# Slot-attention column sums as half-precision matmuls in three passes

## The reference, cut to what matters

```python
for _ in range(NUM_ITERS):                      # 3
    sn = rmsnorm(slots, slot_norm_w)
    q_proj = sn @ Wq.T
    scores = jnp.einsum('bkd,bmd->bkm', q_proj, k_proj) * SCALE
    attn = jax.nn.softmax(scores, axis=-2)      # over the slots (tokens) k
    attn = attn / (jnp.sum(attn, axis=-1, keepdims=True) + EPS)   # over the context rows m
    updates = jnp.einsum('bkm,bmd->bkd', attn, v_proj)
    slots = gru_cell(updates, slots, gru_wih, gru_whh, gru_bih, gru_bhh)
```

## Time and profile before

| | us |
|---|---|
| median of 3 runs | 910.36 |
| lowest, highest | 908.17, 910.95 |
| the profiled execution's own time | 910.25 |
| its span in the trace | 909.0 |
| PE, DVE, ACT, POOL busy | 879.0, 649.0, 557.5, 365.4 |

### The profile page before, as it was taken

How to read it: one execution, slowest core, us unless ns; L and a number is a source line. 1 busy time by engine, 2 the same in 40 slices (tenths; PEclk the granted TensorE clock), 3 DMA queues, 4 the chain that set the end, 5 groups by cost and what they waited for, 6 DMA issues and landing times. The chain is left out here.

```text
span 909.0 us, 23841 instructions
## 1 busy us (share of the span) xinstructions
PE 879.0 (97%) x8190; PEld 670.8 (74%) x8190; DVE 649.0 (71%) x1839; ACT 557.5 (61%) x1347; POOL 365.4 (40%) x492
## 2 busy tenths in 40 slices
PE   5999999999999999999999999999999999999996
PEld 4777777777777777776666666666788888888864
DVE  4767688777676778667878787769677767776755
ACT  5777877777666677657575654645455545554555
POOL 2333434333323455325444442354534444444433
PEclk9999999999999999999999999999999999999999
DMA  9742434342323241230000000099443332333226
GB/s 320 193 140 94 147 107 153 106 140 94 133 75 123 96 158 49 9 93 1 1 1 2 1 1 2 17 361 409 134 113 50 49 49 44 49 49 48 42 29 191
DMA packets 61584, 88.09 MB, mean 97 GB/s; under 512 B 17279, under 2 KB 46527, under 8 KB 61343
## 3 DMA queue, kind: packets, MB, share of 16 engines
q1 hardware_dynamic: 53439, 75.52, 25.2%
q0 software_dynamic: 7488, 10.27, 7.1%
q10 hardware_dynamic: 544, 0.79, 0.3%
HBM read 56.00 MB, written 30.56 MB: 95 GB/s over the span
## 5 line engine op out<-in xcount | busy, mean ns | idle before, releaser
L2254 PE MATMUL ps<-slots,e 128*128 128x128 f16 x1872 | 189.9, 219 | 2.3 <-DVE xs L2421 2.2
L667 POOL TENSOR_SCALAR prob<-prob,rden 128x128 f32<-128x128 f32 (+1 forms) x256 | 110.6, 448 | 202.6 <-DVE rden L956 202.6
L2254 PEld LDWEIGHTS ps<-slots,e 128*128 x1872 | 152.4, 97 | 35.4 <-issue 5.0
L853 ACT ACTIVATE prob<-prob,nmx 128x128 f32<-128x128 f32 (+1 forms) x256 | 114.1, 450 | 41.6 <-DVE nmx L949 38.9
L2262 PE MATMUL ps<-e,xT 128*128 x312 | 117.3, 378 | 0.0
L2351 ACT ACTIVATE slots<-slots 128x512 f32<-128x512 f32 x78 | 49.0, 630 | 106.9 <-DVE slots L2405 103.1
L31 PE MATMUL ps<-xT,wqkv 128*128 128x256 f16 x768 | 97.2, 278 | 0.6 <-DVE wqkv L936 0.6
L31 PEld LDWEIGHTS ps<-xT,wqkv 128*128 128x128 f16 x768 | 70.9, 99 | 30.5 <-issue 22.2
L2263 PE MATMUL ps<-e,xT 128*128 x312 | 85.0, 273 | 0.0
L1766 POOL DMA_INDIRECT xg<-rows_x,dst x39 | 40.9, 1049 | 106.3 <-DVE mask L2394 103.2
L949 DVE CUSTOM_DVE_ANT_0 prob<-ps,mask 128x128 f32<-128x128 f32 (+1 forms) x256 | 75.9, 353 | 5.0 <-PE ps L747 5.0
(11 more groups left out here) (275 smaller groups left out, 1940.5 us busy)
## 6 DMA issues: line engine op xcount, KB each, us to landing
halves<-parted SPq DMA_DIRECT2D x36, 512.0 KB, 2.9
piece<-in_L_ffn_ew SPq DMA_DIRECT2D x32, 512.0 KB, 4.4
e<-halves SPq DMA_DIRECT2D x16, 1024.0 KB, 15.4
piece<-in_L_ffn_sh_w SPq DMA_DIRECT2D x4, 512.0 KB, 8.8
sw<-halves SPq DMA_DIRECT2D x4, 512.0 KB, 6.7
rows_x<-xs SPq DMA_DIRECT2D x4, 512.0 KB, 7.1
xs<-back_y SPq DMA_DIRECT2D x8, 256.0 KB, 5.9
out<-xs SPq DMA_DIRECT2D x8, 256.0 KB, 2.1
```

The source lines that it names most:

```text
L667: PO.tensor_scalar(prob[m % 3][:, h, r], prob[m % 3][:, h, r], rden[m % 2][:, h, t:t + 1], 1.0, ALU.mult, ALU.mult).then_inc(normed, 1)
L853: SC.activation(p, p, ACT.Exp, bias=nmx[u][:, h, t:t + 1], scale=-1.0, accum_out=den[u][:, h, t:t + 1]).then_inc(exped, 1)
L2254: yield PE.matmul(ps[:, 2 * u + q, (k % 4) * P:(k % 4) * P + P], w[ch][h], xgT[u][j][:, ch, :], start=n == 0, stop=n == 3 * DC - 1)
```

## The change

The column sums of steps 1 to 11 are made from half-precision parts. ACT makes `exh[0]`, the exponentials times 2^15 rounded to float16, in one operation on 120 x 512 (`exponentials_high`), behind the r gate of chunk 0 and before the z gate. DVE makes `exh[1]`, what the rounding left, in one operation with two SBUF inputs (`exponentials_low`), at the head of step n before `reset(n, 0)`. DVE also cuts `grec` in two parts, two small operations more in `denominators`. PE then does 3 products for each of the 4 tiles: 12 one-column float16 matmuls in place of 4 float32 ones. On PE the column sums move from between the two halves of the r gate of chunk 1 to behind it. `cse` takes the scale out again. The counts of `g_exp` and `g_rec` follow. The column sum of step 0 stays as it was.

```diff
--- before.py
+++ after.py
@@ -1200,6 +1200,8 @@
         with ExitStack() as c:
             sh.extend([sb(c, f"s{i}{g}", [P, DC, GT], F16) for i in range(2)] for g in range(2, NG))
             sqh = [sb(c, f"sqs{i}", [P, GT], F16) for i in range(2)]
+            exh = [sb(c, f"ex{i}", [P, GT], F16) for i in range(2)]
+            grech = [sb(c, f"grec{i}", [P, BG], F16) for i in range(2)]
             rr = sb(c, "rr", [P, GT])
             sc = sb(c, "sc", [P, BG, S])
             ex = sb(c, "ex", [P, BG, S])
@@ -1222,6 +1224,21 @@
             g_neg, g_exp, g_rec = (sem(k) for k in ("g_neg", "g_exp", "g_rec"))
             cs_mm, c_eps2, c_rec, c_cut, cb_mm = (sem(k) for k in ("cs_mm", "c_eps2", "c_rec", "c_cut", "cb_mm"))
             SUM_UP = 32.0
+            EX_UP, GREC_UP = 2.0 ** 15, 2.0 ** 8
+            def exponents_made(n):
+                return BG * (n + 1) + max(0, n - 1)
+            def exponents_high(n):
+                return BG * (n + 1) + n
+            def inverted(n):
+                return 5 * n - 3 if n else 0
             an_out, an_hi, an_lo = (sem(k) for k in ("an_out", "an_hi", "an_lo"))
             r_mm, z_mm, hn_mm, xn_mm = (sem(k) for k in ("r_mm", "z_mm", "hn_mm", "xn_mm"))
             tr_out, tz_out, hn_out, nn_out = (sem(k) for k in ("tr_out", "tz_out", "hn_out", "nn_out"))
@@ -1258,15 +1275,22 @@
                     mm.then_inc(sc_mm, 1)
 
                 def column_sums(n):
-                    PE.wait_ge(g_rec, 2 * n + 1)
+                    PE.wait_ge(g_rec, inverted(n) + (5 if n else 1))
+                    if n >= 1:
+                        PE.wait_ge(g_exp, exponents_high(n))
                     if n + 1 < STEPS:
                         PE.wait_ge(r_msq, meaned(n + 1))
                     if n >= 1:
                         PE.wait_ge(c_eps2, n)
                     for t in range(TG):
                         k = t * P // S
-                        mm = PE.matmul(ps[:, 6, TG + t:TG + t + 1], exf[:, t * P:t * P + P], grec[0:M, k:k + 1],
-                                       start=True, stop=True)
+                        if n == 0:
+                            mm = PE.matmul(ps[:, 6, TG + t:TG + t + 1], exf[:, t * P:t * P + P], grec[0:M, k:k + 1],
+                                           start=True, stop=True)
+                        else:
+                            mm = split_matmuls(PE, ps[:, 6, TG + t:TG + t + 1], [
+                                ([exh[i][0:M, t * P:t * P + P] for i in range(2)],
+                                 [grech[i][0:M, k:k + 1] for i in range(2)])])
                     mm.then_inc(cs_mm, 1)
 
                 def sums_along(n):
@@ -1299,10 +1323,10 @@
                     else:
                         PE.wait_ge(tr_out, m)
                     from_hidden(n, 0, ch, False)
+                    PE.wait_ge(an_lo, n + 1)
+                    from_update(n, 0, ch, False).then_inc(r_mm, 1)
                     if ch == 1 and n + 1 < STEPS:
                         column_sums(n + 1)
-                    PE.wait_ge(an_lo, n + 1)
-                    from_update(n, 0, ch, False).then_inc(r_mm, 1)
 
                 def gates_z(n, ch):
                     m = 2 * n + ch
@@ -1396,6 +1420,12 @@
                         SC.activation(ex[0:M, k, :], sc[0:M, k, :], ACT.Exp, bias=gneg[0:M, k:k + 1],
                                       accum_out=gden[0:M, k:k + 1]).then_inc(g_exp, 1)
 
+                def exponentials_high(n):
+                    SC.wait_ge(g_exp, exponents_made(n))
+                    if n >= 2:
+                        SC.wait_ge(cs_mm, n)
+                    SC.mul(exh[0][0:M, :], exf, EX_UP).then_inc(g_exp, 1)
                 def weights(n):
                     SC.wait_ge(an_out, BG * (n + 1))
                     if n >= 2:
@@ -1445,6 +1475,8 @@
                 sums_high(2)
                 for n in range(STEPS):
                     gate_r(n, 0)
+                    if n + 1 < STEPS:
+                        exponentials_high(n + 1)
                     if n == STEPS - 1:
                         norm_high(0)
                     gate_z(n, 0)
@@ -1534,7 +1566,7 @@
                     VE.wait_ge(rr_out, n + 1)
                     VE.wait_ge(sc_mm, n + 1)
                     if n >= 1:
-                        VE.wait_ge(g_exp, BG * n)
+                        VE.wait_ge(g_exp, exponents_made(n - 1))
                     for k in range(BG):
                         VE.tensor_tensor_reduce(sc[0:M, k, :], ps[0:M, 5, k * S:(k + 1) * S],
                                                 rr[0:M, k * S:(k + 1) * S], 1 / WS, LOWEST, ALU.mult, ALU.max,
@@ -1543,18 +1575,32 @@
                     VE.tensor_scalar(gneg[0:M, :], gmx[0:M, :], -1.0, None, ALU.mult).then_inc(g_neg, 1)
 
                 def denominators(n):
-                    VE.wait_ge(g_exp, BG * (n + 1))
+                    VE.wait_ge(g_exp, exponents_made(n))
                     if n >= 1:
                         VE.wait_ge(an_out, BG * n)
                     VE.reciprocal(grec[0:M, :], gden[0:M, :]).then_inc(g_rec, 1)
-                    VE.wait_ge(g_rec, 2 * n + 1)
+                    VE.wait_ge(g_rec, inverted(n) + 1)
                     VE.tensor_scalar(grec_up[0:M, :], grec[0:M, :], SUM_UP, None, ALU.mult).then_inc(g_rec, 1)
+                    if n >= 1:
+                        if n >= 2:
+                            VE.wait_ge(cs_mm, n)
+                        VE.tensor_scalar(grech[0][0:M, :], grec[0:M, :], GREC_UP, None, ALU.mult).then_inc(g_rec, 1)
+                        VE.wait_ge(g_rec, inverted(n) + 3)
+                        VE.scalar_tensor_tensor(grech[1][0:M, :], grec[0:M, :], GREC_UP, grech[0][0:M, :], ALU.mult,
+                                                ALU.subtract).then_inc(g_rec, 1)
+                def exponentials_low(n):
+                    VE.wait_ge(g_exp, exponents_high(n))
+                    if n >= 2:
+                        VE.wait_ge(cs_mm, n)
+                    VE.scalar_tensor_tensor(exh[1][0:M, :], exf, EX_UP, exh[0][0:M, :], ALU.mult,
+                                            ALU.subtract).then_inc(g_rec, 1)
 
                 def column_sums(n):
 
                     VE.wait_ge(cs_mm, n + 1)
-                    VE.tensor_scalar(cse[:, :], ps[:, 6, TG:2 * TG], SUM_UP, SUM_UP * SUM_EPS, ALU.mult,
-                                     ALU.add).then_inc(c_eps2, 1)
+                    VE.tensor_scalar(cse[:, :], ps[:, 6, TG:2 * TG], SUM_UP / (EX_UP * GREC_UP) if n else SUM_UP,
+                                     SUM_UP * SUM_EPS, ALU.mult, ALU.add).then_inc(c_eps2, 1)
                     VE.wait_ge(c_eps2, n + 1)
                     if n >= 1:
                         VE.wait_ge(c_cut, 3 * n)
@@ -1569,7 +1615,7 @@
 
                 def weights(n):
                     VE.wait_ge(cb_mm, n + 1)
-                    VE.wait_ge(g_rec, 2 * (n + 1))
+                    VE.wait_ge(g_rec, inverted(n) + 2)
                     if n >= 1:
                         VE.wait_ge(an_hi, n)
                         VE.wait_ge(an_lo, n)
@@ -1626,6 +1672,8 @@
                 sums_low(2)
                 mean_square(2)
                 for n in range(STEPS):
+                    if n + 1 < STEPS:
+                        exponentials_low(n + 1)
                     if n == STEPS - 1:
                         norm_low(0)
                     reset(n, 0)
```

## The result

| | median us | lowest, highest | runs |
|---|---|---|---|
| before | 909.85 | 908.17, 911.94 | 15 |
| changed | 913.50 | 910.55, 915.16 | 15 |

Ratio 1.0039, 95% interval 1.0031 to 1.0047: the change makes the kernel slower by 3.6 us, where +1.35 was forecast. The profiled execution of the changed kernel took 910.88 us (span 909.5), one of its fastest; before's took 910.25.

The account below looks back on a forecast made before the run. A ring of ACT, DVE and POOL, 15.27 us a step, bounds the kernel, not PE. 910.25 - 0.25 + 0.45 + 1.15 = 911.6 us; own range 910.1 to 913.5, set to 907.3 to 915.5 for scatter.

Parts of the forecast that it names:

- What sets the pace: Slot steps: a chain of ACT, DVE and POOL, period 15.27 us, sets the pace; PE follows with 0.3 us to spare.
- the ring: Closed chain of ACT, DVE and POOL operations from one step's z gate to the next, no matmul in it; 15.27 us.
- PE's wait for L470: At `root_along` each step: PE's saved 0.49 us becomes waiting, 0.78 us where it was 0.3.
- Rival 1: PE sets the pace after all, so all 11 savings count: -5.4 us, 904.9 us; chance 0.11.
- PE's slot: Column sum on PE each step: twelve one-column matmuls take 0.32 us instead of 0.81, saving 0.49.
- Step 0: PE bounds step 0, so there the column-sum saving counts: -0.25 us.
- The push on reset: In step 0, `exponentials_low(1)` ahead of reset(0, 0) pushes it by 0.1 to 0.2 us.
- `exponentials_low` behind the power: Steps 1 to 9: POOL's power L462 delays this DVE operation, pushing reset 0.05 us a step: +0.45 us.
- Rival 2: Steps 1 to 9: POOL's power keeps DVE out of SBUF until it ends, +0.61 a step; 916.7 us, chance 0.17.
- Step 10: Later `cse` puts L1567 behind POOL's dl, where it stands and delays `norm_sum(0)` and PE: +1.15 us.
- rival 3: Step 10: L1567 is not held, as dl shifts too or an on-time DVE candidate moves it; 910.6 us, chance 0.14.
- the wait of PE in step 11: PE's 1.04 us wait for POOL's L1500 grows, as all of step 10's 1.15 us delay arrives at PE.

Follow-up runs that it names:

- four_more: The kernel before with 4 more unused one-column float16 matmuls ahead of the float32 column sums of steps 0 to 9; ratio to before 1.0036.
- old_place_10: The changed kernel with step 10's column sum back between the halves of the r gate; 910.20 us, ratio to before 1.0008.
- filled_wait: The changed kernel with 18 unused 256-column matmuls where PE waits 2.5 us in step 11; 910.99 us, ratio to before 1.0015.
- the three padded kernels: 80 or 256 waits heading PE's list in before (1.0012; 256 one run), 80 in the half-precision kernel with slots - nn on DVE (0.9927).
- the two kernels with the shorter chain: slots - nn of steps 0 to 10 on DVE, not POOL: on before (ratio 0.9994), and on the changed kernel with step 10's old order (0.9934).

## Why the prediction came out as it did

What sets the pace: right. The period stayed at 15.27 in every kernel in which dl is made by POOL, with 0.5 us less on PE (changed), with 0.1 more (four_more), and it moved only when the ring was shortened. PE's wait for L470 grew by 0.50 us a step, for a saving of 0.50 (0.49 was forecast). Rival 1 is out.

PE's slot: 0.31 for 0.32, so a one-column pair takes 0.31 / 12, about 26 ns. The prediction took the 8-column row for the nearest one, which was a misreading: the kernel before has one-column float16 matmuls at L441, eight of them in 0.20 us (478.10 to 478.30), 25 ns each. The 81 ns that the Trainium skill ("TensorE: Matmul & The Clock Gate", section "Back-to-back issue gap") has for 128 columns, and that would have given 0.97, was not for this case: the table of the same section has about 25 ns for 1 to 64 columns, and the trace agrees.

Step 0: -0.44 us on the start of step 1's z gate, for -0.25. The push on reset that I had allowed for did not show.

`exponentials_low` behind the power: the term of 0.45 us was too large, it is 0. L1596 took 0.69 with the power in flight. Rival 2 is out. The rule on which it rested (the Trainium skill, "SBUF — State Buffer", section "Who interferes with whom") agrees with dl against L470 (1.23 us for 4 elements) and not with the power. The cast, which has one SBUF input and not two, was held by dl as well (1.09).

Step 10: its period grew by 1.06 us for a forecast of +1.15, but by another instruction, so that the size came out right by luck in part. I had L1567 stand; it was the cast two operations before it. And rival 3 had it wrong that a candidate on time would spare the block: it was on time, dl moved ahead with it, and the block came. In before the 0.46 us gap had held dl back just far enough.

The sum of these is +0.6 us in the traces (S 176.28 to 176.84), not +1.35, and the measurement is +3.6. So the sum had two terms too few. One is shown: the wait of PE in step 11, which I priced at its own length only, is in most executions followed by 3.4 us at half clock, 1.6 us more. old_place_10 and filled_wait take it away by two different edits and gain 3.1 and 2.3 us. In the profile before, had the row (PE idle 1.04 us, to become 2.2) and I did not ask what a longer idle time does to the clock. The other is X, 1.1 us longer in the changed kernel, 0.8 of it in G. The prediction had no term for a stage that the change does not touch. There the fetch of a 16 KB piece on q8 falls at 1.94 us and not 3.59, into the gather, whose last packets come 0.7 us later. Edits of PE's list alone (four_more and the three padded kernels) moved the fetch, and the end of the gather with it. That the gather's last packets stand behind this fetch is read from their times (the 4.23 and 4.24 us of four_more) and was not tested by itself; the 0.3 us of X outside G stay open.

The terms seen in the traces, 0.6 + 1.6 + 1.1, make 3.3 of the 3.6 us. So the direction (slightly slower) held, and so did the mechanism of the steps. But the sum was 1.9 us short of the median, 913.5 is the very edge of the forecast's own range, and the time lay well inside only because I had widened that range to 915.5 for the scatter of the runs: that part is luck. One late DVE cast set off 1.1 us in step 10 and 1.6 us of half clock behind it, 2.7 us together.

## What to carry to other kernels

An engine that is busy 97% of the time can still follow another chain. Look for a wait of this engine that comes back in every round, and for a closed chain on the other engines in which each link starts when the one before it ends. What is taken from the busy engine then turns into a longer wait. When a change lengthens an idle time of PE, price the clock behind it too. When it lengthens an engine's list of instructions, look at where the fetches of that list fall in later stages. A saving that is hidden is not lost: shorten the chain first, then it pays (here 0.49 us a step; the two kernels with the shorter chain lie 5.7 us apart, in part by the clock).

## What was not expected of the hardware

A cast of 4 elements a partition, from SBUF to SBUF on DVE, took 0.95 to 1.24 us instead of 0.17 behind a POOL subtraction of 128 x 512 in four kernels, but an operation with two SBUF inputs ran beside POOL's power of 128 x 4 (1.45 us) at its plain 0.69. The same 2.5 us wait of PE was followed by full clock in one execution and by 3.4 us at half clock in another. Forty to 256 more entries in PE's list moved a 16 KB instruction fetch by up to 2.7 us against a gather, far behind the place of the edit, and with it the end of the gather by up to 1.8 us.
